# ScalarE writes the mask's terms into the score banks, and a step's scores stand behind its values and down half

## The reference

```
xn = ln(x, g_norm)
q = l2norm(xn @ Wq) * q_scale          # 16 heads of 64
k = l2norm([null_k; xn @ Wk]) * k_scale; v = [null_v; xn @ Wv]      # one k, v for all heads
sim = 8 * q @ k.T + [null_bias; rel_pos_bias]
sim = where(causal, -max, sim)
sim = where(mask, sim, -max)           # mask of the input: one flag for each key
x1 = x + ln(softmax(sim) @ v @ Wout, g_out)
p = leaky(x1 @ sw_gate) * (x1 @ sw_up) @ sw_down
moe = sum over top 2 of 8 experts of w_e * ((leaky(x1 @ gate_e) * (x1 @ up_e)) @ down_e) + p
```

## Time and profile before

| | |
|---|---|
| time, median of 3 runs | 1048.13 us (1047.93 to 1050.3) |
| the profiled execution, its own time | 1048.86 us |
| its span | 1047.1 us |
| TensorE busy | 1006.9 us, 96% |
| TensorE weight loads | 811.3 us, 77% |
| VectorE busy | 703.5 us, 67% |
| ScalarE busy | 523.6 us, 50% |
| GpSimd busy | 437.4 us, 42% |
| mean granted TensorE clock | 0.997 of full speed |
| chain that ended last | PE 83%, DVE 8%, issue 2%, ACT 2% |

### The profile page before, as it was taken

The page is one execution under the profiler, slowest core; times in us unless marked ns, Lnnn a source line. Parts: engine busy times, 40 slices in busy tenths (PEclk is TensorE's granted clock), DMA queues, the critical chain, the costliest instruction groups (busy, mean ns, idle before and its releaser), DMA issues.

```text
span 1047.1 us, 19955 instructions
## 1 busy us (share of the span) xinstructions
PE 1006.9 (96%) x6774; PEld 811.3 (77%) x6774; DVE 703.5 (67%) x2459; ACT 523.6 (50%) x1556; POOL 437.4 (42%) x422
## 2 busy tenths in 40 slices
PE   3878999999999999999999999999999999999998
PEld 2656977778777887778777797777877788777877
DVE  8887677765867558674777657676586755856553
ACT  3588256652566345662466615655256633565220
POOL 1645155443364344451545415454335434444212
PEclk9999999999999999999999999999999999999999
DMA  5220305121331112321132212321133111232042
GB/s 201 78 75 2 125 7 172 62 92 61 102 102 61 62 41 90 104 71 42 61 105 69 71 62 61 113 71 42 61 98 105 62 41 42 86 107 72 22 141 101
DMA packets 39539, 82.21 MB, mean 79 GB/s; under 512 B 4032, under 2 KB 18880, under 8 KB 39184
## 3 DMA queue, kind: packets, MB, share of 16 engines
q1 hardware_dynamic: 38480, 78.32, 22.8%
q10 hardware_dynamic: 960, 2.62, 0.7%
HBM read 71.33 MB, written 9.60 MB: 77 GB/s over the span
## 4 chain that ended last, share of the span: by engine, by line
PE 83%; DVE 8%; issue 2%; ACT 2%; DVEq 0%; POOL 0%
PE psY L1685 14%; PE psS L1552 7%; PE psG L70 6%; PE psG L72 6%; PE psG L71 6%; PE psO L1588 6%; PE psT L1563 5%; PE psS L1548 3%; PE psS L71 3%; PE psS L70 3%; PE psS L72 3%; PE psT L1570 2%; PE psO L1591 2%; PE psT L70 2%; PE psT L72 2%
## 5 line engine op out<-in xcount | busy, mean ns | idle before, releaser
L634 POOL TENSOR_TENSOR work<-work,rden 128x514 f32<-128x514 f32 x128 | 134.3, 1049 | 313.8 <-DVE rden L1179 313.8
L1685 PE MATMUL psY<-Wd,H 128*128 128x256 f32 x640 | 171.7, 397 | 0.0
L782 ACT ACTIVATE work<-work,low 128x257 f32<-128x257 f32 x256 | 128.3, 502 | 54.7 <-DVE low L1197 53.7
L70 PE MATMUL psG<-x1T_hi,Wgu 128*128 128x512 f32 (+1 forms) x292 | 134.7, 461 | 2.1 <-ACT leaky L826 1.9
L1685 PEld LDWEIGHTS psY<-Wd,H 128*128 128x128 f32 x640 | 111.7, 189 | 29.0 <-issue 14.6
L1197 DVE CUSTOM_DVE_ANT_0 work<-psS,bias,null_s 128x256 f32<-128x256 f32 x256 | 113.2, 479 | 24.3 <-PE psS L1552 22.8
L1293 DVE SCALAR_TENSOR_TENSOR leaky<-leaky 128x512 f32<-128x512 f32 x80 | 57.0, 713 | 103.2 <-ACT leaky L826 102.3
L623 POOL TENSOR_TENSOR rq<-qss,neghalf 128x16 f32<-128x16 f32 x32 | 97.6, 3050 | 43.8 <-DVE qss L1173 43.8
L72 PE MATMUL psG<-x1T_lo,Wgu 128*128 128x512 f32 (+1 forms) x292 | 114.5, 392 | 0.0
L71 PE MATMUL psG<-x1T_hi,Wgu 128*128 128x512 f32 (+1 forms) x292 | 114.0, 390 | 0.0
L1552 PE MATMUL psS<-KB,qT 64*128 64x256 f32 (+1 forms) x1024 | 105.8, 326 | 0.0
(11 more groups left out here) (262 smaller groups left out, 2288.9 us busy)
## 6 DMA issues: line engine op xcount, KB each, us to landing
Wgu<-wexp SPq DMA_DIRECT2D x70, 512.0 KB, 3.4
Wb<-wscr SPq DMA_DIRECT2D x64, 256.0 KB, 3.7
wexp<-Wgu SPq DMA_DIRECT2D x10, 512.0 KB, 3.3
xres<-in_x SPq DMA_DIRECT2D x8, 512.0 KB, 3.8
xin<-in_x SPq DMA_DIRECT2D x7, 512.0 KB, 4.5
out<-work SPq DMA_DIRECT2D x7, 512.0 KB, 3.0
raw<-in_wgu SPq DMA_DIRECT2D x10, 256.0 KB, 4.6
bias<-bscr SPq DMA_DIRECT2D x4, 512.0 KB, 5.9
```

What stands on the lines that cost most here:

```text
L70: te.matmul(dst, a_hi, b_hi, start=start, stop=False)
L634: pool.tensor_tensor(T1[sl][:, hs, :], T1[sl][:, hs, :], rden[sl][:, 1, hs].unsqueeze(2) .to_broadcast([P, 2, N + 1]), ALU.mult)
L782: act.activation(T1[sl][:, h, :], T1[sl][:, h, :], ACT.Exp, scale=-1.0, bias=low[sl][:, 1, h:h + 1], accum_out=den[sl][:, 1, h:h + 1])
L1685: mm = te.matmul(psY[:, t // 2, (t % 2) * D:(t % 2 + 1) * D], H[:, k % H_RING, t * P:(t + 1) * P], Wd[:, ORDER[k], :], start=(k == 0 and t ...
```

## The change

In rounds 1 to 7 and for n > 0, M goes away. In its place ScalarE copies `MK` (bf16, 128x384, once for each of the two banks) into `psS` for step n+1, between the two pairs of exponentials of step n, behind its wait for `s0_read`; it signals `mask_ps`. For this `MK` must hold the mask in all 128 partitions, so the mask is loaded with two DMAs that spread it over the partitions, not with four that each fill one. S of step n > 0 now waits for `mask_ps` alone, adds to what lies in the banks, and stands behind V, the q transposes and D of its step and ahead of G and T. Round 0 and n = 0 stay as they are.

```diff
-        mask_in = events("mask_in", 64)
+        mask_in = events("mask_in", 32)
...
+        mask_ps = events("mask_ps", ALL - 1)
...
-                for i in range(2):
-                    for a, b in ((0, N), (N, P)):
-                        sp.dma_start(mask8[i * DH:i * DH + 1, :, a:a + b],
-                                     mask[:, bass.ds(r * TOK, TOK)].rearrange("a (b j) -> a b j", b=BB)[:, :, 0:b]) \
-                            .then_inc(mask_in.sem, 16)
+                for a, b in ((0, N), (N, P)):
+                    sp.dma_start(mask8[:, :, a:a + b],
+                                 mask[:, bass.ds(r * TOK, TOK)].rearrange("a (b j) -> a b j", b=BB)[:, :, 0:b]
+                                 .to_broadcast([P, BB, b])).then_inc(mask_in.sem, 16)
...
+            def put_mask(r, n):
+
+                act.activation(psS[:, :, 0:N + P], MK[:, n // STEPS // 2, :].unsqueeze(1).to_broadcast([P, 2, N + P]),
+                               ACT.Copy).then_inc(mask_ps.sem, 1)
...
                 need(act, s0_read, r, n + 1)
+                if moe is not None and n + 1 < ALL:
+                    put_mask(r, n + 1)
                 for h in (2 * s, 2 * s + 1):
...
-                    if n < ALL:
-                        score(r, n // STEPS, n % STEPS)
+                    if n < ALL and (n == 0 or moe is None):
+                        score(r, n // STEPS, n % STEPS, moe)
...
+                        if 0 < n < ALL:
+                            score(r, n // STEPS, n % STEPS, moe)
                         if n in GATE_AT:
                             gate(moe, GATE_AT[n], fresh=fresh)
...
-                need(te, s1_read, r, n)
-                need(te, s0_read, r, n)
-                for i in range(2):
-                    half = slice(i * DH, (i + 1) * DH)
-                    te.matmul(psS[:, i, 0:N + P], pick_bf[half, :], MK[half, bb, :], start=True, stop=False)
+                added = moe is not None and n > 0
+                if not added:
+                    need(te, s1_read, r, n)
+                    need(te, s0_read, r, n)
+                    for i in range(2):
+                        half = slice(i * DH, (i + 1) * DH)
+                        te.matmul(psS[:, i, 0:N + P], pick_bf[half, :], MK[half, bb, :], start=True, stop=False)
+                else:
+                    need(te, mask_ps, moe, n)
```

More of the change, by code:

```diff
@@ L758, in attention @@
                     if n < ALL:
-                        exps(r, n // STEPS, n % STEPS)
+                        exps(r, n // STEPS, n % STEPS, moe)
                     if moe is not None and n in GATE_AT:
@@ L775, in head_out, with exps @@
                                ACT.Copy).then_inc(o_lead.sem, 1)
-            def exps(r, g, s):
+            def put_mask(r, n):
+                act.activation(psS[:, :, 0:N + P], MK[:, n // STEPS // 2, :].unsqueeze(1).to_broadcast([P, 2, N + P]),
+                               ACT.Copy).then_inc(mask_ps.sem, 1)
+            def exps(r, g, s, moe):
                 sl = g % 2
@@ L1034, in attention @@
                 ins.then_inc(kd_done.sem, 1)
-                need(dve, mask_in, r, 64)
+                need(dve, mask_in, r, 32)
                 dve.tensor_scalar(MK[:], mask8[:], -BIG, BIG, ALU.mult, ALU.add).then_inc(mk_done.sem, 1)
@@ L1536, in attention, with score @@
                     q_first(following)
-            def score(r, g, s):
+            def score(r, g, s, moe):
                 bb, p = g // 2, STEPS * (g % 2) + s
@@ L1552, in score @@
                         mm = te.matmul(psS[:, i, first:first + keys_], qT[half, p, q1:q1 + P], KB[half, bb, 0:keys_],
-                                       start=False, stop=(first == N))
+                                       start=False, stop=(first == N or added), skip_group_check=added)
                 mm.then_inc(s_ps.sem, 1)
```

## The result

The changed kernel takes 1113.97 us (median of four runs, 1113.6 to 1115.13) against 1048.13: the ratio is 1.0625, with a 95% interval of 1.0607 to 1.0643, so it is 6% slower. Forecast were 1103 us and a range of 1062 to 1118. The profiled execution took 1115.13 us by its own time, over a span of 1113.3; before it was 1048.86, so 66.3 us have to be found.

What follows compares the result with a forecast made beforehand. TensorE, busy 119.4 of 120 us, was taken to bound the kernel. Changes of shape (+9) and waits (46) add 55 to the profiled 1048.86, giving 1104, as a median 1103 us; range 1062 to 1118.

Steps and rivals of the forecast that it cites:

- A change of shape costs 0.20, a full step +0.14: TensorE empties before a new array shape: 0.20 into D, S or G; four changes for three lengthen full steps by 0.14.
- the forecast's signs: Rows expected in the new profile, among them the weight port idle ahead of S and G by 0.12 to 0.2.
- The forecast's five pieces: A full step on TensorE: S 0.85, G 1.50, T 0.75, V 0.81, D 1.06, given as 4.96.
- The copy at 0.81: ScalarE's copy of 768 elements per partition into PSUM takes 0.81 us, ends 0.59 and 1.03.
- V at steps 9 and 16: Behind steps 8 and 15, which lack G, V waits 1.35 each for `o_done`, which VectorE gives behind `scores`.
- V at step 13: `norm_x` after step 11 delays `scores` of step 12, so `head_out` is late and V waits 2.4, in six rounds.
- the copy's waits: Waits at steps 2 to 4 through the added ScalarE copy, 1.35 us a round in all.
- S of step 4 waits 0.3: `leak` holds VectorE, so `scores` of step 3 starts 0.8 late and S of step 4 waits 0.3.
- Loads ahead across shapes: Rival: S's and G's weights load ahead despite new shapes, M's 28 us are won, waits remain: 1076; chance 0.10.
- `o_done` in time: Rival: VectorE gives V its signal in time, only changes of shape cost: 1058, or 1048 without copy's waits; chance 0.06.
- The rival of no 0.15 to spare: V's thin margin in full steps fails as ScalarE runs late: 0.3 in 63 places, 1122; chance 0.07.
- The second rival: The case of `o_done` in time: 1058 with the copy's waits of 9, 1048 without; chance 0.06.

Runs made afterwards that it cites:

- experiment 4: Changed kernel with S behind V but ahead of D, ScalarE's copy kept: 1070.44 us, ratio 1.0214.
- Experiment 3: Changed kernel without the copy: mask product stays on TensorE, M and S together behind V and D: 1106.4 us, ratio 1.0553.
- Experiment 1: Changed kernel with VectorE reading the values' result (`head_out`) ahead of a step's `scores`: 1108.17 us, ratio 1.0571.
- experiment 5: Changed kernel with GpSimd weighing expert block 2 at step 1, not step 2, ahead of scaling pair 1: 1105.12 us, ratio 1.0534.
- Kernel 10: As kernel 9, but S behind V and ahead of D in steps 5 to 14: 1039.98 us, ratio 0.9912.
- kernel 9: Kernel before with ScalarE's copy from step 5 on, S in its old place, `norm_x` two tiles each at steps 11 and 13 ahead of `leak`: 1042.74 us.
- Kernel 11: Kernel before with only `norm_x` moved, two tiles each at steps 11 and 13 ahead of `leak`: 1044.45 us, ratio 0.9956.
- experiment 2: Changed kernel with ScalarE's copy but S in its old place at the beginning of its step: 1072.58 us, ratio 1.0247.

## Why the prediction was right

- *TensorE bounds, and each wait is paid in full.* Right. From S of step 0 to that of the next round it is 134.3 us from round 1, 133.65 to 133.8 from rounds 2, 4 and 5, and 135.2 from rounds 3 and 6, against 124.6 before: 58.3 of the 66 in six distances. The last round, which has no `norm_x`, gives 6.9, and the start 1.0: in round 0 the granted clock stood at its half from 53 to 60 us, before from 56 to 59.
- *A change of shape costs 0.20, a full step +0.14.* Right: 4.97 from V to V, 4.96 from S to S where V doesn't wait, against 4.82; the 0.2 came back when D and S changed places (experiment 4). The port's idle time ahead of S was 0.33, not the 0.12 to 0.2 of the forecast's signs. The forecast's five pieces add to 4.97, not to its 4.96.
- *The copy at 0.81.* 0.79 measured. S of step 3 waits 0.60 by its port (0.93 less 0.33; 0.6 forecast), the up product of step 3 0.43 (0.35), S of step 2 nothing (0.1).
- *V at steps 9 and 16.* 1.36 each (1.35 forecast). Experiment 3 shows it without a copy. Experiment 1 shows that it is one of several chains: without it, waits of S, G and T on other chains take most of its place.
- *V at step 13.* 2.5 where 2.4 was forecast. The number is partly luck: V itself waits 1.5, and T's part of 1.0, for `turned` behind `norm_x`, was not in the prediction. The two small waits of V, 0.3 at step 8 and 0.2 at step 10, were 0.14 and 0.09 by the length of the steps.
- *The term that was mis-sized* is what was booked as the copy's waits, 1.35 a round; 2.7 was measured. "S of step 4 waits 0.3" was the wrong end of that chain: D of step 4 waits 1.65 (the port's 1.67 less the usual 0.02) for GpSimd ahead of it, and S behind D finds its copy ready. I followed the late `leak` to `scores`, not to `rdens`, from which GpSimd starts. That is 1.35 a round more, 9 us, and experiment 5 gives it back: 9 us. It isn't the copy's wait either: experiment 3 has it without a copy (1.65 in the port's row against 1.67), so it belongs to the move. The waits of a round are then 2.7 and, for V and T, 5.4, together 8.1 where 6.95 was forecast. Over the rounds (the last has no `norm_x`) that is 54, not 46, and the sum on the profiled execution 1112, not 1104.
- *The rest*, 3 us to the measured 1115, is made of small terms that the prediction did not have: the half clock in two rounds, told below, 3.2; the start, 1.0; V of step 10 in round 1, 0.6, which was not followed further; and less 1.8, since in six rounds the kernel before has a wait of its own of 0.3 ahead of M of step 13 (5.12 from S to S there, 4.82 in the last round), which the forecast did not take off.
- *The rivals.* Loads ahead across shapes: refuted by the 0.33 ahead of S and by experiment 4. `o_done` in time: refuted by the rows of step 9. The rival of no 0.15 to spare: V waits 0.01 to 0.04 in full steps, not 0.3, so the margin was all but gone. The second rival's price was added wrongly: with the 9 of the changes of shape it is 1057 without the copy's waits and 1067 with them, not 1048 and 1058.

The Trainium skill's rule of "TensorEngine Tiling (Array Packing)", Key Properties, that changing the tiling mode drains TensorE, agrees with the 0.17 and 0.33 of idle port at the changes of shape. The Trainium skill's rule of "TensorE: Matmul & The Clock Gate", Step-by-step: what each phase is for, that loads for the background buffer are pulled ahead of matmuls in flight, held from D to G before, which have one shape (the port went on after 0.03), and not from D to S after (it idled for 0.33).

Kernel 10 is 2.8 us faster than kernel 9 by the medians, but the two profiled executions lie only 1.5 apart (1041.88 and 1040.41). A round is 123.77 in kernel 9 and 123.54 in kernel 10, and 0.23 is what S of step 6 waits for the copy in kernel 9 (its port's 0.40 less 0.17) and not in kernel 10. The other 1.3 us of the medians has no rows here and stays open.

## What to carry to other kernels

Work that is taken from the engine that bounds is worth what it frees in that engine's own row of starts, with the changes of array shape on either side: here a mask product of 0.27 freed 0.06 a step where three changes of shape were left (4.76 against 4.82), and cost 0.15 where a fourth came (4.97 against 4.82). Moving a piece later in an in-order loop shortens the way between it and everything in the next step that depends on its readers, so list each chain that starts at it (scores, copy, exponentials, `turned`, `rdens` and GpSimd, `head_out`) and look at the shortest steps, where a piece is missing. A new wait that is taken away alone may give nothing if another chain from the same late start is as long.

## What was not expected of the hardware

The granted clock of TensorE fell inside rounds 1 to 7, which it did not before. Windows view of the changed kernel (busy us of each engine, granted clock, DMA share) around step 13 of round 3, and in the same place of round 6:

```profile
480.00:483.00 3.00, 3.00 (x19) 2.24 (x18) 2.72 (x6) 0.99 (x3) 1.75 (x2) 1.00 0.25 97
483.00:486.70 3.70, 1.50 (x12) 1.02 (x12) 3.50 (x17) 2.04 (x7) 0.43 (x1) 0.98 0.43 142
486.70:490.10 3.40, 3.40 (x13) 2.17 (x13) 0.00 (x0) 1.31 (x6) 2.41 (x3) 0.52 0.00 0
490.10:493.50 3.40, 3.40 (x22) 2.58 (x23) 1.78 (x9) 2.33 (x8) 0.00 (x0) 1.00 0.00 0
889.60:892.90 3.30, 3.30 (x13) 2.16 (x12) 0.10 (x1) 1.08 (x4) 2.18 (x3) 0.52 0.00 0
```

TensorE was busy for 1.50 of 3.70 us, in the longest wait of the round; then 3.4 us ran at 0.52 of full speed, the 1.2 GHz level, though it was busy for all of them; then the clock was back at 1.00. It happened in two of the six rounds that have this wait, and makes these two 1.6 us longer than rounds 2 and 4. Why these two and not the others stays open.

Round 0 of the kernel before has the same at its steps 12 and 13, where `norm_x` makes T and then M wait (0.49 and 1.14 in their rows). Windows view of it, the end of the wait and what follows:

```profile
88.00:89.70 1.70, 0.56 (x6) 0.40 (x6) 1.70 (x11) 1.02 (x5) 0.01 (x1) 1.00 0.00 0
89.70:93.20 3.50, 3.50 (x21) 2.50 (x18) 2.14 (x11) 2.23 (x10) 1.60 (x2) 0.51 0.01 2
```

Kernel 11 has neither: from S of step 12 to S of step 14 of round 0 it is 5.6 us, where it was 8.6. In rounds 1 to 6 the low stretch came at that step, in one execution of each kernel, in two rounds of the changed kernel, three of experiment 5's, two of experiment 2's and one of experiment 4's. It never came in experiment 3's, where the step is 1.7 us longer than its neighbours, nor in experiment 1's, where the wait of 2.3 us is split in two. Rounds 1 to 7 of kernels 9 to 11, which have no such wait, show no low stretch. So a wait of TensorE can be paid a second time, and not in every round.
